# Whole history groups in one transfer, masks of four pairs in one, and targets split in time: a target-attention kernel on one core

## The reference

```python
q = (target_item @ W_q).reshape(b, H, HD)
k = (history_sequence @ W_k).reshape(b, S, H, HD)
v = (history_sequence @ W_v).reshape(b, S, H, HD)
scores = jnp.einsum('bhd,bshd->bhs', q, k) / SCALE
scores = jnp.where(mask[:, None, :] == 0, NEG, scores)
attn = jax.nn.softmax(scores, axis=-1)
out = jnp.einsum('bhs,bshd->bhd', attn, v).reshape(b, A)
return out @ W_o
```

## Time and profile before

| what | value |
|---|---|
| median of 3 runs | 579.4 us |
| profiled execution, device time | 578.07 us |
| its span, first to last instruction | 576.1 us |
| PE busy | 538.1 us (93%) |
| DVE busy | 504.2 us (88%) |
| ACT busy | 291.3 us (51%) |
| POOL busy | 309.2 us (54%) |
| DMA | 219.04 MB, 380 GB/s over the span |
| mean granted clock of PE | 0.993 |

### The profile page before, as it was taken

The page is one execution under the profiler, slowest core; times in us unless marked ns, Lnnn a source line. Parts: engine busy times, 40 slices in busy tenths (PEclk is TensorE's granted clock), DMA queues, the critical chain, the costliest instruction groups (busy, mean ns, idle before and its releaser), DMA issues.

```text
span 576.1 us, 41624 instructions
## 1 busy us (share of the span) xinstructions
PE 538.1 (93%) x18604; PEld 437.8 (76%) x18604; DVE 504.2 (88%) x577; ACT 291.3 (51%) x949; POOL 309.2 (54%) x1126
## 2 busy tenths in 40 slices
PE   5597999999999999999999899999999999999996
PEld 4475878778787877877787787878778787877875
DVE  5657899999999899999998999999999999999970
ACT  2053545554555555455555545545554554555453
POOL 6653456465655556565555556556465645646500
PEclk9799999999999999999999999999999999999999
DMA  8967999999999999999999999999999999999950
GB/s 327 416 259 278 354 406 411 402 405 405 412 404 409 405 406 405 405 413 398 410 406 403 385 395 408 406 403 409 405 405 405 409 402 399 410 407 401 402 213 7
DMA packets 47687, 219.04 MB, mean 380 GB/s; under 512 B 5696, under 2 KB 14416, under 8 KB 47648
## 3 DMA queue, kind: packets, MB, share of 16 engines
q1 hardware_dynamic: 46368, 217.35, 94.8%
q0 software_dynamic: 704, 1.05, 0.5%
q10 hardware_dynamic: 576, 0.25, 0.2%
HBM read 217.58 MB, written 1.05 MB: 380 GB/s over the span
## 4 chain that ended last, share of the span: by engine, by line
PE 71%; DVE 17%; DMA 5%; issue 5%; SPq 1%; ACT 0%; DVEq 0%; POOLq 0%; POOL 0%
PE ps_s L251 27%; PE ps_c L281 23%; DVE blocks L475 15%; PE ps_p L264 7%; PE ps_y L291 6%; PE ps_u L239 3%; PE ps_u L298 3%; DMA x_t<-r_target_item 3%; DMA hist<-r_history_sequence 2%; DVE probs_t L496 1%; SPq L153 1%; PE ps_y L306 1%; ACT p_pad L410 0%; DVE inv_sum L491 0%; SPq L144 0%
## 5 line engine op out<-in xcount | busy, mean ns | idle before, releaser
L475 DVE STREAM_TRANSPOSE blocks<-hist 128x768 f32<-128x768 f32 (+2 forms) x320 | 472.1, 1494 | 25.4 <-DMA hist<-r_history_sequence 23.2
L199 POOL COPY u_pad<-u_sb 32x32 f32<-32x32 f32 x1024 | 236.3, 231 | 111.6 <-ACT u_sb L389 53.7
L251 PE MATMUL ps_s<-blocks,u_pad 128*32 128x200 f32 x4096 | 193.7, 335 | 16.5 <-DVE blocks L475 14.4
L281 PE MATMUL ps_c<-hist,p_pad 64*32 64x128 f32 x12800 | 199.8, 271 | 4.0 <-issue 3.1
L281 PEld LDWEIGHTS ps_c<-hist,p_pad 64*32 64x32 f32 x12800 | 181.8, 105 | 19.8 <-issue 17.3
L410 ACT ACTIVATE p_pad<-ps_p,own 128x200 f32<-128x200 f32 x512 | 170.1, 443 | 42.4 <-PE ps_p L264 42.4
L251 PEld LDWEIGHTS ps_s<-blocks,u_pad 128*32 128x32 f32 x4096 | 122.8, 109 | 72.2 <-issue 26.5
L203 POOL TENSOR_SCALAR bias<-mask 128x200 f32<-128x200 int32 x64 | 56.5, 883 | 128.1 <-DMA mask<-r_mask 127.7
L419 ACT COPY ctx_sb<-ps_c 128x128 f32<-128x128 f32 x128 | 27.8, 269 | 88.5 <-PE ps_c L281 88.5
L393 ACT ACTIVATE probs<-neg_score,neg_max 128x200 f32<-128x200 f32 x64 | 29.4, 459 | 81.2 <-DVE neg_max L484 81.1
L264 PE MATMUL ps_p<-probs_t,place_sel 128*64 128x112 f32 x1024 | 63.7, 267 | 0.8 <-DVE probs_t L496 0.5
(11 more groups left out here) (42 smaller groups left out, 93.0 us busy)
## 6 DMA issues: line engine op xcount, KB each, us to landing
hist<-r_history_sequence SPq DMA_DIRECT2D x128, 832.0 KB, 8.6
hist<-r_history_sequence SPq DMA_DIRECT2D x128, 768.0 KB, 5.9
mask<-r_mask SPq DMA_DIRECT2D x64, 100.0 KB, 8.6
out<-out_sb POOLq DMA_DIRECT2D x21, 48.0 KB, 5.3
x_t<-r_target_item SPq DMA_DIRECT2D x1, 976.0 KB, 16.1
w_in<-L_rec_W_k ACTq DMA_DIRECT2D x1, 64.0 KB, 2.0
w_in<-L_rec_W_q SPq DMA_DIRECT2D x1, 64.0 KB, 2.2
w_in<-L_rec_W_v ACTq DMA_DIRECT2D x1, 64.0 KB, 6.7
```

What stands on the lines that cost most here:

```text
L199: pool.tensor_copy(to, source[Q * c:Q * c + Q, a]).then_inc(u_pad_ready, 1)
L251: mm = pe.matmul(ps_s[ring][Q * b:Q * b + Q, 0:S].rearrange("p (t j) -> p t j", j=J), u_pad[ring][:, i, b, c, :], blocks[slot][:, :, c, J ...
L281: mm = pe.matmul(ps_c[alpha][at:at + Q, 0:D], p_pad[rows, t + par, i, :], hist[2 * ring + i][rows, t + par, :], start=(t == 0), stop=(t + ...
L475: dve.transpose(blocks[g % BLOCKS][:, t0:t1].rearrange("p t c k -> p (t c k)"), hist[g % SLOTS][:, t0:t1, :].rearrange("p t d -> p (t d)") ...
```

## The change

Three things change.

1. **Masks.** One transfer brings the masks of four pairs (128 partitions x 3200 bytes) into one of two buffers. It is issued behind the loads of pairs 0, 2, 6, 10 and so on.
2. **Targets.** All targets but the first 96 came in one load of 976 KB, for which PE waited ahead of the loop. Now 384 columns (`SOON`) come behind the history of pair 0, and `combine` waits for them; the rest comes behind pair 2, and ACT waits for it in the fifth `copy_combined`.
3. **History.** From pair 1 on, each group comes in one transfer of 1600 KB in place of 768 KB and 832 KB. It waits for the whole context of pair p - 3, and the first turn of a group waits for the whole group.

```diff
-        mask_sb = [sb(f"mask{n}", [P, S], I32) for n in range(RING)]
+        mask_sb = [sb(f"mask{n}", [P, BATCHED, S], I32) for n in range(2)]
...
-            def load_mask(p):
-                wait(sp, bias_ready, p - RING + 1)
-                rows = mask[p * Q:(p + 1) * Q, :]
-                sp.dma_start(mask_sb[p % RING][:, :],
-                             rows.unsqueeze(1).broadcast_to([Q, H, S])).then_inc(mask_loaded[p % RING], 16)
+            def load_mask(n):
+
+                wait(sp, bias_ready, BATCHED * (n - 1))
+                rows = mask[n * Q:(n + 1) * Q, :]
+                sp.dma_start(mask_sb[n % 2][:, :, :].rearrange("p k s -> p (k s)"),
+                             rows.unsqueeze(1).broadcast_to([Q, H, BATCHED * S])).then_inc(mask_loaded[n % 2], 16)
...
-                for h, (t0, t1) in enumerate(HALVES):
+
+                for h, (t0, t1) in enumerate(HALVES if p == 0 else ((0, T),)):
                     for i in range(2):
                         g = 2 * p + i
 
-                        wait(sp, ctx_done, 2 * (p - RING) + h + 1)
+                        wait(sp, ctx_done, 2 * (p - RING) + 2)
...
-                    if i == 1 and h == 0 and p == 0:
-                        load_mask(0)
-                if p + 1 < NP:
-                    load_mask(p + 1)
-                if p == 1:
-                    sp.dma_start(x_t[:, ROUND:B], target_t[:, ROUND:B]).then_inc(rest_loaded, 16)
+                if p == 0:
+                    load_mask(0)
+                    sp.dma_start(x_t[:, ROUND:SOON], target_t[:, ROUND:SOON]).then_inc(soon_loaded, 16)
+                if p % BATCHED == 2 and p + 2 < NP:
+                    load_mask(p // BATCHED + 1)
+                if p == 2:
+                    sp.dma_start(x_t[:, SOON:B], target_t[:, SOON:B]).then_inc(late_loaded, 16)
...
                 if not isinstance(r, int):
+                    pe.wait_ge(soon_loaded, 16)
                     pe.wait_ge(u_copied, r)
...
-            pe.wait_ge(rest_loaded, 16)
             warm(WARM[1])
...
                 act.wait_ge(u_done, r + 1)
+                if (r + 1) * ROUND == SOON:
+
+                    act.wait_ge(late_loaded, 16)
...
-                dve.wait_ge(hist_loaded[g % SLOTS][half], 16 * (g // SLOTS + 1))
+                if p == 0:
+                    dve.wait_ge(hist_loaded[g % SLOTS][half], 16)
+                elif half == 0:
+                    dve.wait_ge(hist_loaded[g % SLOTS][0], 16 * (g // SLOTS + 1))
```

More of the change, by code:

```diff
@@ L38, in target_attention @@
     WARM = (5, 4, 3)
+    BATCHED = 4
+    SOON = 5 * ROUND
     assert D == P and GROUP * J == P and S == T * J and NP == RING * LOOPS + 1
@@ L92, in target_attention @@
         x_loaded = sem("x_loaded")
-        rest_loaded = sem("rest_loaded")
+        soon_loaded = sem("soon_loaded")
+        late_loaded = sem("late_loaded")
         x_zero = sem("x_zero")
         hist_loaded = [[sem(f"hist_loaded{n}_{h}") for h in range(2)] for n in range(SLOTS)]
-        mask_loaded = [sem(f"mask_loaded{n}") for n in range(RING)]
+        mask_loaded = [sem(f"mask_loaded{n}") for n in range(2)]
         out_stored = sem("out_stored")
@@ L201, in mask_bias @@
             def mask_bias(p):
-                pool.wait_ge(mask_loaded[p % RING], 16 * (p // RING + 1))
-                pool.tensor_scalar(bias[p % 2][:, :], mask_sb[p % RING][:, :], 0.0, BIG,
+                n = p // BATCHED
+                pool.wait_ge(mask_loaded[n % 2], 16 * (n // 2 + 1))
+                pool.tensor_scalar(bias[p % 2][:, :], mask_sb[n % 2][:, p % BATCHED, :], 0.0, BIG,
                                    ALU.is_equal, ALU.mult).then_inc(bias_ready, 1)
@@ L530 @@
         if name == "r_mask":
-            a = a.reshape(-1, 2, 4, 4, 8, 25).transpose(0, 3, 1, 2, 5, 4).reshape(-1, 200)
+            a = a.reshape(-1, 4, 2, 4, 4, 8, 25).transpose(0, 4, 2, 3, 1, 6, 5).reshape(-1, 800)
         if name in ("r_target_item", "L0_rec_W_q", "L0_rec_W_k", "L0_rec_W_v"):
```

## The result

The changed kernel takes 778.63 us (median of 4 runs, 777.2 to 782.76) against 578.49 us before: a ratio of 1.345 (1.341 to 1.349). The direction was right. The forecast of 710 us and its range up to 765 were too low.

The account below looks back on a forecast made before the run. No engine had slack; a chain of mostly PE work set 8.37 us a pair. A 699.1 us span, 2.0 outside it, 1.3 for median against profiled run, 3 for masks and 5 for disturbances gave 710 us, range 685 to 765.

Parts of the forecast that it names:

- X(q) is at least X(q-2) + 10.3 + 10.7: Loop: context end of pair q trails that of q-2 by at least 21.0 us, where it was 16.75.
- The two terms: Loop: 10.3 us from issue to the second group's landing, then 10.7 us of work to the next context's end.
- sign of being wrong: Loop: history sooner than 10 us after a context's end, or waits sitting with PE and not DVE.
- the first rival: PE's long gaps in the loop: clock falls every time, 3 us for each of 31, 798 us; chance 0.08.
- disturbances: Loop: 5 us added, within 0 and 45, for disturbed landings and PE's clock falling in long idle stretches.
- The start: Before the loop: PE's 5.8 us wait for all targets goes; 3.4 us won, between 2 and 5.
- X(0): End of pair 0's context: 34.4 us, where it was 37.85.
- X(2): End of pair 2's context: 55.9 us, including 0.3 us for the first passage of PE's code.
- The sum: Whole kernel: 55.9 plus thirty double steps of 21.0 plus 13.2, a span of 699.1 us before additions.
- Masks: Loop: four-pair mask transfers delay history 0.5 us once in eight pairs, at most 4 us, taken as 3.
- A smaller loss: Loop: only the last turn follows the second group's landing; 8.7 us a pair, about 598 us; chance 0.07.
- in time: Loop: second group lands within 6.0 us of context end, so not slower, about 562 us; chance 0.03.

Follow-up runs that it names:

- wide2: The changed kernel with two 512-column matmuls of no use ahead of every place: 721.81 us.
- short_wide1: wide1 with only 20 of each group's 25 history items loaded from pair 3 on: 667.25 us.
- early_fine: The changed kernel with history loaded and waited for in halves as before, keeping the new masks and targets: 582.98 us.
- early_coarse: early_fine with the first turn of a group waiting for both its halves: 725.56 us.
- wide1: The changed kernel with one 512-column matmul of no use ahead of every place: 760.1 us, spread 740.8 to 772.7.
- masks_only: The kernel before with masks of four pairs in one transfer and nothing else: 583.41 us.
- late_fine: early_fine with both halves of a pair issued only when the whole context of pair p - 3 is done: 606.67 us.
- targets_only: The kernel before with the targets split as in the change and nothing else: 580.44 us.
- reordered: The changed kernel with the first group's turns and the previous pair's turned weights ahead of the second group's turns in DVE's list: 707.0 us.

## Why the prediction was wrong, point by point

**The loop held.** "X(q) is at least X(q-2) + 10.3 + 10.7" is what the changed kernel does: 10.6 and 10.9 us when the clock is up (wide2), and when only the first term is changed the time follows it one to one (short_wide1). The two terms were 0.3 and 0.2 us too small. The landing was worked out from two 768 KB loads and 416 GB/s; whole groups took 10.4 us in the rows above and 10.6 in the median. 30 double steps of 0.5 us are 16 us. The two causes that I had in one term come apart in the experiments: the later issue costs 24 us alone, the coarse wait 95 us at the full clock, and together they cost 20 more than the sum (wide2 against early_fine, 139 us). Neither sign of being wrong came: no pair of the loop landed sooner than 10.2 us after X, and DVE's waits for history grew to 183 us.

**The clock was mis-priced.** This is the step that failed. I had the mechanism as the first rival, with gaps of 4.2 us against the single fall of the trace of before 3.7 us after PE stopped, but gave it 0.08 and 5 us (with disturbances) in the sum, on the ground that it was one event and that part of the half clock would lie in idle time. The trace shows a stretch at the half clock in every double step: what came right behind the gap was the critical work, place to scores. The contexts are 8.3 to 8.5 and 13.6 to 16.7 us apart in turn, where I had 8.4 and 12.6. Cost: (762.7 - 61.6) - (706.5 - 60.4) = 55 us over the 30 double steps; wide2's time is 57 us lower. The rival's 798 us was nearer to 778.6 than the forecast, but its price of 3 us for a fall was too high: a double step loses 1.8 us to it. A gap that a change makes recurs with the loop, so the question was whether each one is like the one that the trace had, not how often it might happen. Gaps of 2.8 us were enough in most of the steps of early_coarse, and 2.2 us in some of wide1.

**The start gave nothing.** I had X(0) at 34.4 and X(2) at 55.9; they are 37.6 and 61.6, 5.7 us later. Place of pair 0 started at 24.71, near the 23.8 of the prediction, but its clock was down already (place 1.76 us), and PE's stops in the first round, for which I put 0.3 us, were 1.2, 3.1 and 0.4:

```profile
24.71 1.76 PE L273 MATMUL ps_p<-probs_t,place_sel 128*64 128x112 f32 x16 [2.68 <-DVE probs_t L510]
...
47.87 2.55 PE L290 MATMUL ps_c<-hist,p_pad 64*32 64x128 f32 x84 [3.06 <-issue]
```

**The sum again.** The span was to be 699.1 us before the additions. 16 (the two terms) + 55 (clock) + 6 (start) = 77, and the measured span is 775.9, 77 above.

**Masks** came out at the right size by luck (3 us, of 0 to 4; masks_only costs 3.5): I had hung it on alternate short steps, which masks_only doesn't have. What they cost in the changed kernel itself no run shows, and the sum above leaves nothing for them.

**The other rivals.** "A smaller loss" (598 us) is close to what late_fine does (607 us); DVE's list with the wait ahead of the second group's first turn spoke against it, and rightly. The landing "in time" would have needed 6.0 us, and took 10.4. The rule that went with it is the Trainium skill's, "DMA: Bandwidth & Descriptors", section Rules for kernel authors: 1 MiB or more in one DMA for the most bandwidth. The traces agree with it in sign only: while the queue was full of whole groups it moved 428 GB/s (16 to 28 us of the changed kernel), and with the smaller pieces 418 (8 to 28 us of the kernel before). That is 2%, some 0.2 us of a landing, and the landing was still longer than the 10.3 us forecast.

## What to carry to other kernels

When a ring of buffers is just deep enough, the size of a transfer isn't a matter of bandwidth but of when the first bytes may be used and when the next slot comes free: write the loop as issue, landing, and all that stands behind the landing in each engine's list, and compare it with the periods that the ring allows. Then look at the idle time that a longer loop gives to PE: here gaps of 4.1 to 4.8 us ahead of critical matmuls brought the half clock behind each of them, and gaps of 2.2 to 3.7 us behind most, so price it in every round and not as an accident. Wide matmuls of no use can hold the clock (two did here, one in part of the steps only), but it pays to take the gap away first.

## What was unexpected of the hardware

- 15 small matmuls more in a loop of three pairs brought the loop's code from memory in every second round: 99 instruction packets on q8 in place of 9, 118 us of PE's stops in 50 places, and 885 us. Six wide ones (wide2) did not. Where the limit lies between them was not tried.
- The first stop of PE in its first passage through the loop was 1.3 us in the kernel before, with the DMA engines at 165 GB/s meanwhile, and 3.7 us in targets_only, with them at 407. That code has to queue beside history would explain this pair, but other runs don't fit: the first stop of late_fine is 3.6 us at 185 GB/s, and that of wide2 2.2 us at 20. What sets the length stays open.
- The half clock came behind all 29 of PE's gaps of 4.1 to 4.8 us in the changed kernel, behind most of those of 2.2 to 3.7 us (in 20 double steps of reordered, 25 of wide1, 26 of early_coarse, of 30 each), and once in the loop of wide2, where two matmuls fill the start of the gap and 1.1 us at most stay idle (not the 1.8 to 3.0 us of wide1's expectation).
